# Second norm's root on ScalarE and VectorE, expert weights formed per tile, eight scatters in one row

## The reference

```python
def _layernorm(x, axis=-1, eps=1e-05):
    m = jnp.mean(x, axis=axis, keepdims=True)
    v = jnp.var(x, axis=axis, keepdims=True)
    return (x - m) / jnp.sqrt(v + eps)
...
t = x.reshape(-1, orig_shape[-1])
logits = t @ Wr + br
gates = jax.nn.softmax(logits, axis=-1)
top_vals, top_idx = jax.lax.top_k(gates, K)            # K = 2 of 8
top_vals = top_vals / top_vals.sum(axis=-1, keepdims=True)
onehot = jax.nn.one_hot(top_idx, E, dtype=t.dtype)
combine = jnp.einsum('tk,tke->te', top_vals, onehot)
for e in range(E):
    h = jax.nn.relu(t @ W1[e] + b1[e])
    y = h @ W2[e] + b2[e]
    out = out + combine[:, e:e + 1] * y
...
h = h + _L0_attn_ref(_layernorm(h, axis=-1), ...)
h = h + _L0_ffn_ref(_layernorm(h, axis=-1), ...)
```

## Time and profile before

| | |
|---|---|
| median of three timed runs | 1499.92 us (1499.58 to 1500.66) |
| the profiled execution | 1500.72 us, of which the span from first to last instruction is 1498.9 us |
| mean granted clock of TensorE | 0.979 of full speed |
| busy in the span | TensorE 1399.7 us (93%), VectorE 1184.3 (79%), ScalarE 1008.2 (67%), GpSimd 788.0 (53%) |
| chain that ended last | TensorE 70% of the span, VectorE 11%, GpSimd 7% |

### The profile page before, as it was taken

One profiled execution on the slowest core, in us unless ns is written; L12 is line 12 of the kernel. 1 busy time (PEld: TensorE's weight loads), 2 busy tenths in 40 slices (PEclk: granted clock), 3 DMA queues, 4 the chain that ended last, 5 costly groups with the idle time before them and its releaser, 6 DMA issues.

```text
span 1498.9 us, 32061 instructions
## 1 busy us (share of the span) xinstructions
PE 1399.7 (93%) x7812; PEld 1121.1 (75%) x7812; DVE 1184.3 (79%) x3231; ACT 1008.2 (67%) x2311; POOL 788.0 (53%) x888
## 2 busy tenths in 40 slices
PE   5899999999999999999998988898987999999993
PEld 4677888888888888888886766666765888888871
DVE  2988898989899898989897688777777766666655
ACT  2677887878887888878786666666654555555540
POOL 1675444444444444444442477767666565665561
PEclk8999999999999999999999999999999999999997
DMA  3422222222222222222224988777755787777779
GB/s 85 154 76 73 88 100 76 91 80 87 87 80 91 76 91 80 101 80 91 79 78 144 297 273 273 219 233 227 223 172 198 279 292 254 249 251 246 243 284 362
DMA packets 180725, 245.76 MB, mean 164 GB/s; under 512 B 32641, under 2 KB 143761, under 8 KB 180657
## 3 DMA queue, kind: packets, MB, share of 16 engines
q1 hardware_dynamic: 159872, 206.57, 41.5%
q0 software_dynamic: 13920, 31.33, 6.4%
q10 hardware_dynamic: 6864, 7.09, 1.4%
HBM read 99.85 MB, written 89.51 MB: 126 GB/s over the span
## 4 chain that ended last, share of the span: by engine, by line
PE 70%; DVE 11%; POOL 7%; issue 7%; DMA 2%; ACT 2%; SPq 1%; DVEq 0%; POOLq 0%; ACTq 0%
PE bank L403 15%; PE bank L405 13%; PE bank L404 13%; PE pair_ps L1690 10%; PE bank L1621 5%; PE bank L1715 5%; POOL sorted_scratch L839 5%; PE pair_ps L1854 1%; PE bank L1611 1%; POOL rstdB L833 1%; PE bank L1789 1%; DMA yearly<-y_scratch 1%; PE pair_ps L405 1%; PE pair_ps L403 1%; PE bank L1629 1%
## 5 line engine op out<-in xcount | busy, mean ns | idle before, releaser
L697 POOL TENSOR_TENSOR prob<-expo,inv 92x368 f32<-92x368 f32 x256 | 205.0, 801 | 394.6 <-DVE inv L1219 394.6
L874 POOL DMA_INDIRECT y_scratch<-ytok,tin x198 | 194.0, 980 | 124.1 <-issue 91.9
L839 POOL DMA_INDIRECT sorted_scratch<-trow,posi x184 | 180.2, 979 | 96.0 <-issue 57.5
L1690 PE MATMUL pair_ps<-z,xnT 128*92 128x368 f32 x512 | 201.3, 475 | 0.0
L1212 DVE TENSOR_REDUCE peak<-pair_ps 92x4 f32<-92x368 f32 x256 | 136.1, 532 | 73.2 <-PE pair_ps L1690 73.1
L1403 DVE SCALAR_TENSOR_TENSOR hid_l<-bank,hid_h 128x512 fp32r<-128x512 f32 (+1 forms) x159 | 103.5, 655 | 93.7 <-ACT hid_h L1040 92.7
L914 ACT ACTIVATE z<-bank 128x368 f32<-128x368 f32 x254 | 121.2, 477 | 63.0 <-PE bank L405 55.9
L953 ACT ACTIVATE w2s<-bank 128x368 fp32r<-128x368 f32 x256 | 122.5, 478 | 47.4 <-PE bank L405 43.0
L960 ACT ACTIVATE expo<-cent 92x368 f32<-92x368 f32 x256 | 130.4, 509 | 31.2 <-DVE cent L1224 28.2
L1040 ACT ACTIVATE hid_h<-bank 128x512 fp32r<-128x512 f32 (+1 forms) x159 | 90.5, 569 | 78.9 <-PE bank L405 78.3
L1239 DVE TENSOR_TENSOR w2s<-bank,w2s 128x368 fp32r<-128x368 f32 x256 | 136.2, 532 | 6.0 <-ACT w2s L953 3.1
(11 more groups left out here) (274 smaller groups left out, 3875.3 us busy)
## 6 DMA issues: line engine op xcount, KB each, us to landing
ax_scratch<-val SPq DMA_DIRECT2D x64, 736.0 KB, 3.8
arow<-ax_scratch SPq DMA_DIRECT2D x92, 512.0 KB
w1t<-w1s SPq DMA_DIRECT2D x53, 512.0 KB, 3.2
w2t<-w2s SPq DMA_DIRECT2D x53, 512.0 KB, 3.0
tin<-sorted_scratch SPq DMA_DIRECT2D x46, 260.0 KB
xin<-in_x_dram SPq DMA_DIRECT2D x32, 372.0 KB
ywide<-y_scratch SPq DMA_DIRECT2D x32, 256.0 KB, 7.2
h_scratch<-hP SPq DMA_DIRECT2D x32, 184.0 KB, 5.1
```

Source lines behind the costliest of these rows:

```text
L697: nc.gpsimd.tensor_tensor(prob[:, k % 2], expo[:, k % 2], inv[:, k % 2].unsqueeze(2).to_broadcast([S, HH, S]), ALU.mult).then_inc(prob_kep ...
L839: pool.indirect_dma_start(out=sorted_dram, out_offset=bass.IndirectOffsetOnAxis(ap=posi[:, q, choice, r:r + 1], axis=0), in_=trow[:, q, ch ...
L874: pool.indirect_dma_start(out=y_dram, out_offset=bass.IndirectOffsetOnAxis(ap=tin[:, b, r, D:D + 1].bitcast(I32), axis=0), in_=ytok[:, b % ...
L1690: mm(score_ps[k % 2][0:S, 0:GT], xnT[:, q, b * S:(b + 1) * S], z[:, b, half * HH:(half + 1) * HH, :], start=True, stop=True).then_inc(scor ...
```

## The change

Three things, all in the second and third part.

The root: `root2` on GpSimd goes. ScalarE takes the square root of `varB` into `devB` (`keep_dev2`), behind the fifth block's copy of the chunk; VectorE takes the reciprocal into `rstdB` (`keep_rstd2`), behind the sixth block's `aT_l`, just ahead of `take_logits`.

The weights: ScalarE's Exp (`keep_gapexp`) goes. `weigh` writes the signed gaps in the rows' last column, in five VectorE instructions where there were seven. In the expert part ScalarE applies a Sigmoid to the tile's column (`keep_gate`, into `gate`, two buffers), behind the read of the expert's number; `weigh_y` waits for it and multiplies by `gate`.

The scatters: all eight of a chunk stand in one row on GpSimd, with waits ahead of the first alone. The last chunk's scatters stay as they were.

```diff
-            def root2(c, q):
-                pool_waits((var2_kept, c + 1), (trow_kept, 2 * c - 2), (mask_kept, c - 1))
-                nc.gpsimd.tensor_tensor(rstdB[:, q], varB[:], power[:], ALU.pow).then_inc(rstd2_kept, 1)
...
                 if after_first:
-                    scatter(c - 1, 1 - q, 0, 3)
-                root2(c, q)
-                if after_first:
-                    scatter(c - 1, 1 - q, 3, 5, (rstd2_kept, c + 1))
-                    scatter(c - 1, 1 - q, 5, 2 * RT, turned(AC))
+                    scatter(c - 1, 1 - q, 0, 2 * RT)
...
-            def keep_gapexp(c):
-                at_least(act, gap_kept, c + 1)
-                A(top[:, 3], top[:, 2], ACT.Exp).then_inc(gapexp_kept, 1)
+            def keep_dev2(c):
+                at_least(act, var2_kept, c + 1)
+                at_least(act, rstd2_kept, c)
+                A(devB[:], varB[:], ACT.Sqrt).then_inc(dev2_kept, 1)
+
+            def keep_gate(m, i, q):
+                b = (q - 1) % XRING
+                at_least(act, tile_in[b], 16 * ((m // XRING if isinstance(m, int) else i - int(q == 0)) + 1))
+                at_least(act, ytok_kept, m - 1)
+                k = rows_of_tile(m)
+                A(gate[:, b % 2, 0:k], tin[:, b, 0:k, D + 1], ACT.Sigmoid).then_inc(gate_kept, 1)
...
-                    if j == 0 and (not isinstance(c, int) or c > 0):
-                        keep_gapexp(c - 1)
...
+                    if j == 4:
+                        keep_dev2(c)
...
                     e = act.value_load(whosei[0:1, n - 1:n] if isinstance(n, int) else whosei[0:1, bass.ds(n - 1, 1)],
                                        min_val=0, max_val=NE - 1)
+                    keep_gate(n - 1, i, q)
...
+            def keep_rstd2(c, q):
+                at_least(dve, dev2_kept, c + 1)
+                at_least(dve, trow_kept, 2 * c - 2)
+                V.reciprocal(rstdB[:, q], devB[:]).then_inc(rstd2_kept, 1)
...
-                at_least(dve, gapexp_kept, c + 1)
+                at_least(dve, gap_kept, c + 1)
...
-                V.tensor_tensor(top[:, 10], top[:, 4], top[:, 5], ALU.is_gt).then_inc(route, 1)
-                V.tensor_tensor(top[:, 11], top[:, 5], top[:, 4], ALU.is_gt).then_inc(route, 1)
-                link(c, V.tensor_scalar(top[:, 6], top[:, 3], 1.0, None, ALU.add))
-                V.reciprocal(top[:, 7], top[:, 6]).then_inc(route, 1)
+                link(c, V.tensor_tensor(top[:, 10], top[:, 4], top[:, 5], ALU.is_gt))
                 V.tensor_scalar(mine, mine, 2 * CT, None, ALU.add)
-                link(c, V.tensor_tensor(top[:, 8:10], top[:, 10:12], top[:, 3].unsqueeze(1).to_broadcast(both), ALU.max))
-                V.tensor_tensor(trow[:, q, :, :, D + 1:D + 2].rearrange("p k r o -> p k (r o)"), top[:, 8:10],
-                                top[:, 7].unsqueeze(1).to_broadcast(both), ALU.mult)
+                link(c, V.tensor_scalar(top[:, 11], top[:, 10], -2.0, 1.0, ALU.mult, ALU.add))
+                V.tensor_tensor(gaps[:, 0], top[:, 11], top[:, 2], ALU.mult)
+                V.scalar_tensor_tensor(gaps[:, 1], top[:, 11], -1.0, top[:, 2], ALU.mult, ALU.mult)
...
                     if j == 5:
+                        keep_rstd2(c, q)
                         take_logits(c, q)
...
                 at_least(dve, yt_done, m + 1)
+                at_least(dve, gate_kept, m + 1)
...
-                                tin[:, b, 0:k, D + 1:D + 2].to_broadcast([P, k, D]), ALU.mult).then_inc(ytok_kept, 1)
+                                gate[:, b % 2, 0:k].unsqueeze(2).to_broadcast([P, k, D]), ALU.mult).then_inc(ytok_kept, 1)
```

More of the change, by code:

```diff
@@ L189, in build @@
         power = sb("power", [P, GB])
+        gate = sb("gate", [P, 2, TR])
         rank = sb("rank", [P, RT, NE])
@@ L264, in build @@
         square = sb("square", [P, RT, D], stack=second)
-        sb("behind_tiles", [P, 1072], stack=second)
+        sb("behind_tiles", [P, 1068], stack=second)
         lgraw = sb("lgraw", [P, RT, NE + 1], stack=second)
@@ L268, in build @@
         varB = sb("varB", [P, RT], stack=second)
+        devB = sb("devB", [P, RT], stack=second)
         rstdB = sb("rstdB", [P, 2, RT], stack=second)
@@ L366, in build @@
             "aT_done", "aTh_kept", "aTl_kept", "proj_done", "h1_kept"))
[L367 to L370, removed]
+        wrc_done, wrc_kept, lean_kept, square_kept, var2_kept, dev2_kept, rstd2_kept, shift_kept = (sem(n) for n in (
+            "wrc_done", "wrc_kept", "lean_kept", "square_kept", "var2_kept", "dev2_kept", "rstd2_kept", "shift_kept"))
+        route, mask_kept, gap_kept, gate_kept, count_done, posi_kept = (sem(n) for n in (
+            "route", "mask_kept", "gap_kept", "gate_kept", "count_done", "posi_kept"))
         trow_kept, res_done, res_kept, goal_kept = (sem(n) for n in (
@@ L394, in build @@
         Z_THEN = {1: 4, 2: 6, 6: 10}
-        NR = 25
+        NR = 22
         block = ctx.enter_context(nc.Block())
@@ L843, in chunk @@
             def chunk(c, i, q, more):
-                def turned(blocks):
-                    blocks += AC * (c + 1)
-                    return aTh_kept, min(blocks, AC * NCH) if isinstance(c, int) else blocks
                 after_first = not isinstance(c, int) or c > 0
                 if after_first:
-                    scatter(c - 1, 1 - q, 0, 3)
-                root2(c, q)
-                if after_first:
-                    scatter(c - 1, 1 - q, 3, 5, (rstd2_kept, c + 1))
-                    scatter(c - 1, 1 - q, 5, 2 * RT, turned(AC))
+                    scatter(c - 1, 1 - q, 0, 2 * RT)
                 if isinstance(c, int) and c < SPARE:
@@ L1064, in chunk @@
                         keep_trow(c, q, 1)
-                        if not more:
-                            keep_gapexp(c)
                     if isinstance(c, int) and 1 <= c <= NE and j == 0:
@@ L1332, in weigh @@
             def weigh(c, q):
-                at_least(dve, gapexp_kept, c + 1)
+                at_least(dve, gap_kept, c + 1)
                 at_least(dve, scattered[q], 16 * 2 * RT * (c // 2) if isinstance(c, int) else 8 * 2 * RT * (c - q))
                 dve.wait_ge(goal_kept, SETUP)
-                both = [P, 2, RT]
                 mine = trow[:, q, :, :, D:D + 1].bitcast(I32)
-                step_no[0] += 2
-                V.tensor_tensor(top[:, 10], top[:, 4], top[:, 5], ALU.is_gt).then_inc(route, 1)
-                V.tensor_tensor(top[:, 11], top[:, 5], top[:, 4], ALU.is_gt).then_inc(route, 1)
-                link(c, V.tensor_scalar(top[:, 6], top[:, 3], 1.0, None, ALU.add))
-                step_no[0] += 1
-                V.reciprocal(top[:, 7], top[:, 6]).then_inc(route, 1)
+                gaps = trow[:, q, :, :, D + 1:D + 2].rearrange("p k r o -> p k (r o)")
+                link(c, V.tensor_tensor(top[:, 10], top[:, 4], top[:, 5], ALU.is_gt))
                 V.tensor_scalar(mine, mine, 2 * CT, None, ALU.add)
-                link(c, V.tensor_tensor(top[:, 8:10], top[:, 10:12], top[:, 3].unsqueeze(1).to_broadcast(both), ALU.max))
-                V.tensor_tensor(trow[:, q, :, :, D + 1:D + 2].rearrange("p k r o -> p k (r o)"), top[:, 8:10],
-                                top[:, 7].unsqueeze(1).to_broadcast(both), ALU.mult)
+                link(c, V.tensor_scalar(top[:, 11], top[:, 10], -2.0, 1.0, ALU.mult, ALU.add))
+                V.tensor_tensor(gaps[:, 0], top[:, 11], top[:, 2], ALU.mult)
+                V.scalar_tensor_tensor(gaps[:, 1], top[:, 11], -1.0, top[:, 2], ALU.mult, ALU.mult)
             def rows_of(c, q):
```

## The result

The changed kernel takes 1481.87 us (median of 4 runs, 1479.49 to 1484.82) against 1500.18 of the kernel before (4 runs): 0.9879 of its time, interval 0.9859 to 0.9899, 18.3 us less. The profiled execution has a span of 1481.2 us, 17.7 less than the profiled one of before.

| stretch | before | after | gained | forecast |
|---|---|---|---|---|
| start to the first `h` | 837.53 | 841.33 | -3.80 | 0 |
| chunk 0 | 11.35 | 12.77 | -1.42 | -1.7 |
| A, chunks 1 to 8, one chunk | 12.62 | 11.57 | 8 x 1.05 = 8.4 | 8 x 0.9 = 7.2 |
| B, chunks 9 to 20, one chunk | 12.80 | 11.93 | 12 x 0.87 = 10.4 | 12 x 0.5 = 6.0 |
| chunk 21 | 15.16 | 12.48 | 2.7 | 2.6 |

What follows compares the result with a forecast made beforehand. Taken to bound: TensorE in the expert stage; in routing, the chain scatter, GpSimd's root, VectorE's steps. Terms -1.7 + 7.2 + 6.0 + 2.6 + 0.5 + 0.2 = 14.8 us off 1500.72 gave 1485.9, stated as 1485; range 1475 to 1495.

Steps and rivals of the forecast that it cites:

- The binding wait: Routing chunk: `shift` waits for GpSimd's root, which starts only behind the third scatter; 0.89 us of idle VectorE.
- my terms for the move: Moving the root off GpSimd: 8 x 0.69 + 12 x 0.5 + 2.6 + 0.5 - 1.7 = 12.9 us.
- The root in A and B: Sqrt on ScalarE, reciprocal on VectorE: `shift` 0.69 us sooner per chunk in 1 to 8, 0.5 in 9 to 20.
- the weighting in B: Two fewer VectorE instructions before the positions: 0.2 us a chunk in chunks 1 to 8, nothing in 9 to 20.
- Chunk 0 and 21: Chunk 0 loses 1.7 us to the Sqrt's table load; chunk 21 gains 2.6 us, no longer waiting for GpSimd's root.
- The scatters at nothing: Eight scatters in a row plus zero rows: 11.4 us of GpSimd under a chunk's 11.74, not the bound.
- The gate at nothing: Expert tiles: number read, address step and gate take 1.13 us, fitting the 1.38 between `hid_h` copies; costs nothing.
- the 0.28 us from which it was to decide: Rival, gate on TensorE's path in 53 expert tiles: 0.35 us late each, 1503.7 us; decides from 0.28 a tile; chance 0.05.
- Contention: Rival: GpSimd's unbroken scatters slow VectorE's small steps and some copies, 0.3 us in 22 chunks, 6.6 us: 1492; chance 0.16.
- TensorE as the bound: Rival: TensorE's busy share limits chunks 1 to 8 to 11.4 us each; 23.5 us gained in all, 1476; chance 0.08.
- My two rows: VectorE's variance step, 0.17 us in chunk 5 and 0.25 in chunk 13, read as stretched while GpSimd issues.
- The total: Whole kernel: terms sum to 14.8 us gained, forecast 1485 us; chance 0.65.

Runs made afterwards that it cites:

- the fastest version: Changed kernel plus an early Sqrt table load, `h` ahead of the next chunk's first `aT_l`, and the second `aT_l` ahead of weighting and positions: 1465.95 us, 0.9768.

## Why the prediction was right, point by point

- **The binding wait** was right: the root on GpSimd held `shift`. Putting it back costs 13.35 us from first to last, where my terms for the move sum to 12.9 (12.4 without the 0.5 of chunk 22, which lies behind the last `h`).
- **The root in A and B** was right in kind. With it back on GpSimd a chunk takes 0.81 us more in A, where I had 0.69, and 0.51 more in B, where I had 0.5. In A I had `shift` at 7.26 us after `h`, it came at 7.12: `aT_l` ended 0.11 sooner than I let it, and the reciprocal began 0.09 before that end. In B I charged the Sqrt 0.15 us between the two copies; the copy behind it starts 0.09 after it (1000.27, 1000.36):

```profile
1000.27 0.25 ACT L1018 ACTIVATE devB<-varB 128x4 f32<-128x4 f32 x1
1000.36 0.65 ACT L981 ACTIVATE aT_h<-bank 128x512 fp32r<-128x512 f32 x1
```

- **The term that was mis-sized is the weighting in B**, "I count as nothing here", and with it B's 6.0, which measured 10.4. Before the change, positions set the time of the first scatter and so of the root, in B as in A; I followed them only to `aT_l` and TensorE. With the root on GpSimd that is worth 0.24 us a chunk of B, some 2.9 us in all; the other 1.5 us by which B came out better than forecast are the three long chunks of before that have no like after.
- **Chunk 0 and 21** were right: 1.42 against 1.7, 2.7 against 2.6.
- **The scatters at nothing** was right; that GpSimd was nearly full in A while the root stood there, I had not seen: I summed its turn only without the root.
- **The gate at nothing** was right, and the 0.28 us from which it was to decide is of the right size: 0.31 more cost 0.02 a tile.
- **Contention** came, but off the path: VectorE's variance step takes 0.26 to 0.33 us in seven of A's eight chunks, 0.17 in all of them before. It has time to spare; from `shift` to the next `h` it is 4.41 us in the chunk shown, before 4.49. On the path it stood before the change, in the 0.34 us step of the weighting. My two rows did not show what I read from them: in both of them, 0.17 and 0.25 us, GpSimd was issuing a scatter (last section).
- **TensorE as the bound** was half right: A lies at 11.57 us, near its 11.4, with 0.3 us of wait left. But 11.4 was no floor: the fastest version runs A in 11.04. My window also held more than A; over seven chunks of A alone TensorE was busy 78.97 us, 11.28 a chunk.
- **The total** came out nearer than its terms: they were 21.5 - 14.8 = 6.7 us too small in the routing stage and after it, and the attention part of this execution took 3.8 us more. Part of the closeness of 1485 is therefore luck.

## What to carry to other kernels

When a short step sits in the queue of an engine that issues long rows, try its place in that queue first: one scatter moved gave 10.8 us here, and moving the step to other engines gave more only because the function that needs another table on ScalarE, the Exp, moved out too. Gains of two edits on one loop don't add: ask for each what it is worth once the other is done. A wait taken away at one instruction may only move to the next one of the same queue: look at the second before you price the first.

## What the runs showed of the hardware that was not expected

- A busy share of 90% was no floor for the time. TensorE was busy 78.97 us in seven chunks of A before (the row below) and 76.91 in the fastest version, with 450 and 451 matmuls. The mean times of the three product matmuls are the same (478, 393 and 394 ns, then 478, 396 and 394), and only those of `turn_h` got shorter (293 to 280 ns). So most of what gave way is that the matmuls, whose ends the profile models, overlap more where TensorE waits less.

```profile
848.88:937.25 88.37, 78.97 (x450) 59.62 (x448) 72.65 (x281) 62.10 (x169) 63.99 (x67) 1.00 0.86 272
```

- A scatter that GpSimd issues stretches VectorE's one-input steps of 128x4 elements only in part of its 0.97 us. In the routing stage of the twelve profiles, all 121 such steps that start 0.1 to 0.4 us after a scatter's start take at most 0.173 us, like those with no scatter near; all 78 that start 0.6 to 0.7 us after it take 0.247 to 0.342. The variance steps of the earlier trace rows start 904.43 - 904.10 = 0.33 us and 1007.12 - 1006.43 = 0.69 us after theirs:

```profile
904.10 0.97 POOL L839 DMA_INDIRECT sorted_scratch<-trow,posi  x1 [0.31 <-issue]
...
1006.43 0.97 POOL L839 DMA_INDIRECT sorted_scratch<-trow,posi  x1 [0.30 <-issue]
```

- The pause of GpSimd between the root and the next scatter hangs on the wait: 0.83 us or more where the scatter waits for the root's semaphore, 0.19 in the run with the root back, where it does not.
- Short ScalarE instructions of 128x4 elements overlap: three in a row put the next one back by 0.31 us, though one alone shows 0.19 to 0.21 us.
